# Octonion feed-forward with autocorrelation attention on one core: the transposing of the next rows moved ahead of the up unit, the normalising to the start of the first down unit

## The reference, cut to what matters

```
xn  = layernorm(x)                                   # x is 2048 rows of 1024 f32
att = rfft autocorrelation of each row of xn, top 6 lags, softmax of their weights,
      sum of the row rolled by those lags
ffn: oct_ternary_linear(xp, W) = einsum('...id,koid->...ko', xp, einsum('jik,jod->koid', S_OCT, ternary(W)))
     h = silu(oct(xn, w_gate)) * oct(xn, w_up);  out = oct(h, w_down)     # 8 x 128 -> 8 x 342 -> 8 x 128
return x + att + ffn
```

## Time and profile before

| | |
|---|---|
| median of three runs | 669.55 us |
| profiled execution | 668.58 us, of it the span 666.7 us |
| PE busy | 563.9 us (85%) |
| DVE busy | 541.4 us (81%) |
| POOL busy | 453.3 us (68%) |
| ACT busy | 357.9 us (54%) |
| mean granted TensorE clock | 0.951 of full speed |

### The profile page before, as it was taken

How to read it: one execution, slowest core, us unless ns; L and a number is a source line. 1 busy time by engine, 2 the same in 40 slices (tenths; PEclk the granted TensorE clock), 3 DMA queues, 4 the chain that set the end, 5 groups by cost and what they waited for, 6 DMA issues and landing times.

```text
span 666.7 us, 15801 instructions
## 1 busy us (share of the span) xinstructions
PE 563.9 (85%) x6416; PEld 508.1 (76%) x6416; DVE 541.4 (81%) x1304; ACT 357.9 (54%) x501; POOL 453.3 (68%) x356
## 2 busy tenths in 40 slices
PE   0365844938999999999999999998999999999767
PEld 0254633827998988888898889897989888999767
DVE  1789778798889968996999698969897889967863
ACT  4467364436746663575458455656564645444420
POOL 2004747455877896799759977797869877987630
PEclk9777968879999999999999999999999999999979
DMA  9410001001013001300112010301030011001101
GB/s 225 105 65 0 1 1 64 1 0 66 32 33 127 2 1 66 124 4 2 65 46 83 2 64 3 127 2 65 2 127 2 32 33 65 2 5 61 64 2 64
DMA packets 10233, 30.63 MB, mean 46 GB/s; under 512 B 912, under 2 KB 4016, under 8 KB 10160
## 3 DMA queue, kind: packets, MB, share of 16 engines
q1 hardware_dynamic: 9200, 28.22, 12.8%
q10 hardware_dynamic: 960, 1.40, 0.9%
HBM read 21.23 MB, written 8.39 MB: 44 GB/s over the span
## 4 chain that ended last, share of the span: by engine, by line
POOL 37%; issue 25%; DVE 16%; PE 15%; ACT 5%; DMA 1%; POOLq 0%; ACTq 0%; SPq 0%; DVEq 0%
POOL hop L957 10%; POOL hs L951 6%; PE acc L318 6%; POOL hs L947 6%; POOL hs L952 6%; POOL hs L946 5%; PE acc L302 5%; PE acc L295 3%; DVE hx L794 2%; DMA xr<-in_x 1%; DVE zx L632 1%; POOL r L922 1%; DVE acc L704 1%; DVE bd L700 1%; DVE wd L646 1%
## 5 line engine op out<-in xcount | busy, mean ns | idle before, releaser
L318 PE MATMUL acc<-wd,hop 114*128 114x128 f16 (+1 forms) x3072 | 178.6, 220 | 8.0 <-DVE hop L767 5.3
L318 PEld LDWEIGHTS acc<-wd,hop 114*128 114x128 f16 (+1 forms) x3072 | 175.6, 98 | 10.0 <-issue 7.2
L946 POOL TENSOR_TENSOR hs<-hx 114x512 f32<-114x512 f32 x47 | 60.1, 1279 | 129.3 <-DVE hx L794 128.4
L957 POOL TENSOR_TENSOR hop<-hs,hop 114x1024 f16<-114x1024 f32 x47 | 100.9, 2147 | 33.5 <-ACT hop L489 33.5
L295 PE MATMUL acc<-xop,wg 128*128 128x256 f16 x768 | 98.2, 285 | 19.5 <-DVE zx L632 9.4
L302 PE MATMUL acc<-xop,wg 128*128 128x256 f16 x768 | 95.0, 279 | 19.8 <-DVE acc L740 14.8
L700 DVE TENSOR_TENSOR bd<-acc,pk 114x256 f32<-114x256 f32 (+1 forms) x112 | 47.0, 420 | 79.3 <-ACT pk L531 57.4
L295 PEld LDWEIGHTS acc<-xop,wg 128*128 128x128 f16 x768 | 77.0, 102 | 33.2 <-DVE zx L632 10.0
L954 POOL TENSOR_TENSOR hop<-hx,hop 114x1024 f16<-114x1024 f32 x47 | 101.1, 2152 | 0.0
L302 PEld LDWEIGHTS acc<-xop,wg 128*128 128x128 f16 x768 | 75.7, 100 | 32.7 <-DVE acc L740 15.9
L502 ACT ACTIVATE hop<-hx 114x1024 f16<-114x1024 f32 x48 | 50.7, 1056 | 91.6 <-DVE hx L794 91.6
(11 more groups left out here) (124 smaller groups left out, 812.3 us busy)
## 6 DMA issues: line engine op xcount, KB each, us to landing
xr<-in_x SPq DMA_DIRECT2D x16, 512.0 KB, 4.8
zx<-in_x SPq DMA_DIRECT2D x16, 512.0 KB, 3.6
out_y<-zx SPq DMA_DIRECT2D x16, 512.0 KB, 2.6
hop<-in_w_down SPq DMA_DIRECT2D x1, 1364.0 KB, 19.0
hop<-in_w_gate ACTq DMA_DIRECT2D x1, 1152.0 KB
hop<-in_w_up SPq DMA_DIRECT2D x1, 1152.0 KB
hop<-in_w_gate ACTq DMA_DIRECT2D x1, 192.0 KB
hop<-in_w_up SPq DMA_DIRECT2D x1, 192.0 KB
```

Of the source, the lines that this page charges most:

```text
L318: last = nc.tensor.matmul(acc[:, n % 4, Y, P * s:P * (s + 1)], hop[0:WIDE[c], halves[g, c][t], form, level, :], wd[0:WIDE[c], slot, c, :], ...
L946: nc.gpsimd.tensor_tensor(hs[:, 4:8:2, :], h[:, 0:4:2, :], h[:, 1:4:2, :], ALU.add)
L957: nc.gpsimd.tensor_tensor(half_of(halves[g, c], NJ + 4 * Y, 1), by_tile(hs[:, 0:4, :]), half_of(halves[g, c], NJ + 4 * Y, 0), ALU.subtract ...
```

## The change

1. In the list, for c = 1 and 2, X moves from behind U(c,0) to directly behind N: G(c,0), N, X, U(c,0), G(c,1), U(c,1).
2. The two instructions of the normalising of the next rows move on ACT from the end of iteration N0 to its start, ahead of the copy of N0's sums. The two dot products (L654, for the bound), which stood one behind each X on DVE, both move ahead of N0's first additions.
3. The round of U(0,0) moves one place later, behind the copy of N0's sums. The other tables keep their places.
4. The down product writes component s of both halves Y side by side (bank s // 2) where each half Y had a bank of its own. The copy, the additions and the result then work on runs of 256 or more columns; the result takes two instructions (896 and 128 columns) where it took three (512, 384 and 128).

```diff
             if c:
                 units += [("N", g - 1, c - 1)]
-            units += [("U", g, c, 0)]
             if c and g < G - 1:
                 units += [("X", g + 1, c - 1)]
+            units += [("U", g, c, 0)]
             units += [("G", g, c, 1), ("U", g, c, 1)]
...
-        dot_at[place["X", g, 0]], dot_at[place["X", g, 1]] = (g, 0), (g, 1)
...
-        late = 6 if g == 0 or c == 2 else 4 if (c, Y) == (0, 0) or (c, Y, g) == (1, 0, G - 1) else 5
+        late = 6 if g == 0 or c == 2 else 4 if (c, Y, g) == (1, 0, G - 1) else 5
+        if g and g < G - 1 and c and Y == 0:
+            late -= 1
...
-                                last = nc.tensor.matmul(acc[:, n % 4, Y, P * s:P * (s + 1)], hop[0:WIDE[c], halves[g, c][t], form, level, :],
+                                at = T * (s % 2) + P * Y
+                                last = nc.tensor.matmul(acc[:, n % 4, s // 2, at:at + P], hop[0:WIDE[c], halves[g, c][t], form, level, :],
...
             for n in range(N + 8):
+                if n in norm_at and n < N and units[n][0] == "N":
+                    normalise(norm_at[n], 0)
+                    normalise(norm_at[n], 1)
                 if n in round_at:
...
+                if n in norm_at and kind == "N":
+                    dot(norm_at[n], 0)
+                    dot(norm_at[n], 1)
                 if kind and kind in "GUNX":
                     first_adds(n, u)
...
-                        nc.vector.scalar_tensor_tensor(res[:, 0, :, :], pair[:, 0, :, :], osc[:, :], res[:, 0, :, :], ALU.mult, ALU.add)
-                        nc.vector.scalar_tensor_tensor(res[:, 1, 0:3, :], pair[:, 1, 0:3, :], osc[:, :], res[:, 1, 0:3, :], ALU.mult, ALU.add)
-                        nc.vector.scalar_tensor_tensor(res[:, 1, 3, :], pair[:, 1, 3, :], nosc[:, :], res[:, 1, 3, :], ALU.mult, ALU.add).then_inc(out_done, 1)
+                        nc.vector.scalar_tensor_tensor(res[:, 0:most], pair[:, 0:most], osc[:, :], res[:, 0:most], ALU.mult, ALU.add)
+                        nc.vector.scalar_tensor_tensor(res[:, most:D], pair[:, most:D], nosc[:, :], res[:, most:D], ALU.mult, ALU.add).then_inc(out_done, 1)
```

More of the change, by code:

```diff
@@ L317, in down @@
                             for level in range(2):
-                                last = nc.tensor.matmul(acc[:, n % 4, Y, P * s:P * (s + 1)], hop[0:WIDE[c], halves[g, c][t], form, level, :],
-                                                        wd[0:WIDE[c], slot, c, :], start=which == 0 and Y not in seen,
-                                                        stop=c == NC - 1 and i == 7 and level == 1, skip_group_check=which == 1)
-                                seen.add(Y)
+                                at = T * (s % 2) + P * Y
+                                last = nc.tensor.matmul(acc[:, n % 4, s // 2, at:at + P], hop[0:WIDE[c], halves[g, c][t], form, level, :],
+                                                        wd[0:WIDE[c], slot, c, :], start=which == 0 and s // 2 not in seen,
+                                                        stop=c == NC - 1 and Y == 1 and i % 4 == 3 and level == 1, skip_group_check=which == 1)
+                                seen.add(s // 2)
                 last.then_inc(spec_mm if which == 0 else term_mm, 1)
@@ L529, in _ @@
                             act.wait_ge(spec_mm, prod_no[u] + 1)
[L530 to L534, removed]
+                            rows = P if kind == "N" else CH
+                            nc.scalar.activation(pk[0:rows, q % 2, :, :], pair[0:rows, :, T:2 * T], ACT.Copy).then_inc(copied, 1)
                     if kind == "F":
@@ L566, in _ @@
                     row_var(*var_at[n])
-                if n in norm_at:
+                if n in norm_at and n < N and units[n][0] != "N":
                     normalise(norm_at[n], 0)
@@ L672, in quad_parts @@
                 rows = pair.shape[0]
[L673 to L680, removed]
+                four = [pair[:, i // 2, T * (i % 2):T * (i % 2 + 1)] for i in range(4)]
+                odd = [pk[0:rows, q % 2, i, :] for i in range(2)]
+                room = [bd[0:rows, q % 2, i, :] for i in range(2)]
                 return four, odd, room
@@ L799, in _ @@
                         _, g, t = v
[L800 to L801 removed]
+                        pair = bank_pair(n - 2).rearrange("p b e -> p (b e)")
+                        res = zx[:, t, :]
+                        most = D - DB
                         dve.wait_ge(term_mm, prod_no[v] + 1)
                         dve.wait_ge(z_done, n_no[v] + 1)
[L804 to L806 removed]
+                        nc.vector.scalar_tensor_tensor(res[:, 0:most], pair[:, 0:most], osc[:, :], res[:, 0:most], ALU.mult, ALU.add)
+                        nc.vector.scalar_tensor_tensor(res[:, most:D], pair[:, most:D], nosc[:, :], res[:, most:D], ALU.mult, ALU.add).then_inc(out_done, 1)
                     elif v[0] == "F":
```

## The result

The changed kernel takes 710.64 us (median of 4 runs, 710.04 to 712.07) against 669.25 us before: 1.0628 times as long, interval 1.0605 to 1.065, so 41.4 us slower. The forecast was 704.0, range 692 to 712. The span went from 666.7 to 708.2 us, +41.5.

What follows compares the result with a forecast made beforehand. It took a loop through the in-order queues of POOL, ACT, DVE and PE, not PE's 67.08 us, as the bound. First stage +5.6, five stages +28.9, group 7 0: +34.5 on 669.55 gives 704.0 us, range 692 to 712.

Steps and rivals of the forecast that it cites:

- rival C: PE's clock falls behind new holes at U(1,1) and U(2,1): twelve falls at 1.3 us, 720 us; chance 0.07.
- The hole ahead of X0: PE's wait for h before X0, 1.18 us a stage; the earlier copy of N0's sums would remove it.
- The loop: One stage from h of U(2,0) to the next, through POOL, ACT and DVE queues: 75.8 us against 70.03.
- Legs 2 to 5: From the result of N0 to h of U(2,0), by DVE and ACT: 7.76, 8.02, 12.99 and 7.76 us.
- leg 1: The POOL part of a stage, h of U(2,0) to the result of N0: 39.26 us.
- The wait for z: DVE waits about 1 us ahead of each result for ACT's z.
- PE's holes: PE waits at U(1,1) and U(2,1) for the banks of N0 and N1: 2.6 to 2.9 us each.
- DVE's 5.78 us: DVE's idle time waiting for the copy of N0's sums; two dot products of 0.61 us would fit there, hidden.
- Group 7: The last group, without X and with its order hardly changed: 0 us, bounds -1.5 and +1.5.
- Bank layout: Down product's component halves side by side: DVE's result pair 1.31 us start to start against 1.44, PE's writes 0.
- Rival A: PE sets the pace and its holes of 2.92 us a stage close: 17.5 us gained, 652 us; chance 0.06.
- Rival B: z does not hold the result, which follows U(c,0)'s first additions on DVE: stages 74.0 us, 693.5 us; chance 0.10.

Runs made afterwards that it cites:

- the short dot products: The changed kernel with its two dot products over 16 columns in place of 512, at the same places: 703.53 us, ratio 1.0519.
- Taking z out: The changed kernel with z one place earlier on ACT, ahead of the round of U(c-1,1) and of L512: 698.14 us, ratio 1.044.
- all three reliefs: The changed kernel with z one place earlier, ACT's copy of U(c,0) before L512, and DVE's second additions ahead of the result: 672.88 us, ratio 1.0065.

## Why the prediction was right

- *Where it landed.* 710.64 lies in the range of 692 to 712, but outside the forecast's own 699 to 709: the 6.6 us between it and 704.0 are two terms that were too small, and the upper end had been drawn towards rival C.
- *The hole ahead of X0 goes, and the copy of N0 comes 3 us earlier.* Right only for what it names. The copy came 2.6 us earlier against PE, at 398.14, ahead of a round that waits until 401.81; the wait for h moved to U(1,0) (1.28 us for 1.18); and DVE's additions gained 0.75 us. The forecast had placed the normalising in the schedule of before, where `rstd` ends at 372.2 and N0's sums are ready at 375.1, 2.9 us later. In the changed kernel it is only 1.5 us (the normalising starts at 395.86, N0's sums are ready near 397.4), so the copy waits for the normalising, and the additions for the dot products. With the order as before, parts 2 to 4 are worth little all the same (stages of 69.4 us against 70.0), since other waits came up.
- *The loop is 75.8 us.* Right. Legs 2 to 5 were 36.64 us for 36.53, leg 1 39.99 for 39.26; with the short dot products the stage measured 75.7. The wait for z was 0.77 where "about 1" stood, PE's holes 2.55 and 2.50 where 2.6 to 2.9 stood. Taking z out gave 74.9, all three reliefs 71.8, the order back 69.4.
- *Two terms of the sum were too small.* The 41.5 us are 34.5 and 7.0 more. First, "the two dot products fit in DVE's 5.78 us, both are hidden". They are not: they put N0's additions 1.86 us behind the copy on DVE, and they hold up POOL by 0.9 us, and these two queues end leg 1 within 0.04 us of each other. 76.62 - 75.8 = 0.8 us a stage, 4 us in five. In the first stage, where the sum has no POOL leg, the two dot products took 0.86 and 2.43 us for 0.68 each,

```profile
166.28 0.86 DVE L657 SCALAR_TENSOR_TENSOR dj<-xr 128x512 f16<-128x512 f32 x1 [0.51 <-ACT xr L438]
...
167.25 2.43 DVE L657 SCALAR_TENSOR_TENSOR dj<-xr 128x512 f16<-128x512 f32 x1
```

  which is 1.9 us on DVE's own path. From F(1)'s last matmuls on, that stage was 7.7 us longer than before (91.69 for 84.02), and 5.9 with the dot products back behind X, where 5.6 were forecast: a run shows this part. Secondly, rival C in part: after the hole at U(1,1) the clock was at half (0.51, the level of 1.2 GHz) in three of five stages, and those three are 77.2 us against 76.6: 0.6 us each, 1.7 in all. The falls at U(2,1) cost nothing: the distance from there to the next opening is 7.62 us with one (212.68 to 220.30, 16 matmuls at 3.57 us) and 7.62 without (367.06 to 374.68). That C would be "mostly hidden" was right; its 1.3 us a time was an upper end.
- *Group 7* was -0.4, within its bounds.
- *Bank layout:* 1.31 us forecast for the result pair; the rows give 414.67 - 413.34 = 1.33, and the layout back cost 0.26 a stage.
- *Rival A* (PE as what sets the pace) fell, and with it the reading of the Trainium skill by which the most contended engine is optimised first (Perfetto Trace Analysis, section Identifying the Most-Contended Engine). That section judges TensorE by the share of its weight loads and not by its matmuls' busy time; that share was 76% before, under DVE's 81%, so the prediction's 85% was not the page's own measure. The sentence of the section Optimization Strategy on gaps that repeat was the right one here: the gap repeats at U(1,1) and U(2,1), and it is the banks of a down unit that are not free. *Rival B* would have been 74.0 a stage; z did hold the result. With z taken out the stage was 74.9, and the 0.9 above B's figure are of the size of the dot products on DVE, which B did not have either; no run tests that.
- Open: through which of its two queues a dot product lengthens leg 1, and how the 16 us between the new order alone and the whole change divide between the late copy and the clock. One run of each kernel was profiled, so how often the clock falls is known from those stages only.

## What to carry to other kernels

In a software pipeline over in-order engines, add up the loop from one action to its own next turn through every queue, not only the busiest engine's work: here PE had 67 us of work in a stage and the loop took 76. When a unit is moved ahead of another, look at what each helper engine now does first, above all a copy that frees nothing until a long chain behind it is through; with the order back, moving that one copy and z was worth 17 us (665.42 to 647.96). And an instruction put into an idle gap of one engine is not free if what it waits for comes late in the new schedule, or if it blocks a second engine that has no gap.

## What the runs showed of the hardware

The dot products on DVE, some small steps of the bound, and POOL's additions took turns by whole instructions. Already in the kernel before, the bound's small steps on DVE, 16 columns each, took 0.16 to 0.17 or 1.13 to 1.19 us:

```profile
614.63 1.17 DVE L662 TENSOR_SCALAR sm<-sm 128x16 f32<-128x16 f32 x1
615.83 0.17 DVE L663 SCALAR_TENSOR_TENSOR sm<-dots,sm 128x16 f32<-128x16 f32 x1
616.04 1.13 DVE L664 TENSOR_TENSOR sm<-sm,dmin 128x16 f32<-128x16 f32 x1
```

```profile
614.50 1.26 POOL L947 TENSOR_TENSOR hs<-hx 114x512 f32<-114x512 f32 x1
615.85 1.29 POOL L951 TENSOR_TENSOR hs<-hs 114x512 f32<-114x512 f32 x1
```

The long ones end 0.03 to 0.04 us after POOL's instruction does (614.50 + 1.26 = 615.76 and 614.63 + 1.17 = 615.80; 615.85 + 1.29 = 617.14 and 616.04 + 1.13 = 617.17). The Trainium skill says the same (SBUF — State Buffer, section "SBUF: two separate sides"): the pair of ports that VectorE and GpSimd share is an exclusive lock, held for the whole instruction. The trace agrees in the taking of turns. The page gives the lock to a VectorE instruction with two SBUF inputs and to one in a two-port mode; L662 is listed with a single tensor input and waited too, and whether it ran in such a mode, no run here shows.

The clock of TensorE: behind holes of 1.7 us or less none of the profiled stages had a group of 16 matmuls that ran long. Behind the holes at U(1,1) and U(2,1) of 2.0 to 3.6 us some had: 3.57 us for 16 at 260.39, behind 2.54 us, and 2.36 and then 3.18 us for the next two groups at 289.85, behind 2.03 us. Others had not, in the same kernel and at the same places: 1.92 us at 414.81, behind 2.55 us, and at 367.06, behind 2.03.
